# Reordered end of attention, and two experts gathering a third batch of rows on TensorE, in a one-core kernel of expert layer, attention and expert layer

## The chip, the core and the metric

One core of one Trainium2 chip runs the whole program. The metric is the device time of one execution in microseconds, the median of several runs. TensorE is written PE, VectorE DVE, ScalarE ACT, GpSimd POOL and SyncE SP, and the DMA queues that SP and POOL feed are theirs.

## The reference

Four sequences of 512 tokens of 128 numbers go through three residual blocks. `layernorm` is over the last axis.

```
x = x + 0.5 * ffn(layernorm(x))      # 8 experts, each token goes to its best one
x = x + attn(layernorm(x))           # 16 heads of 64, causal, tanh on q, k, v and on the output
x = x + 0.5 * ffn(layernorm(x))      # the same experts and weights again

ffn(t):                              # 2048 tokens, capacity 320 tokens an expert
    probs = softmax(t @ gate_w.T);  e = argmax(probs)
    rank  = how many earlier tokens chose e;  kept if rank < 320
    h = relu(t @ w1[e] + b1[e]);  y = h @ w2[e] + b2[e]
    return probs[e] * y if kept else 0
attn(t):
    q, k, v = tanh(t @ Wq + bq), tanh(t @ Wk + bk), tanh(t @ Wv + bv)
    p = softmax(causal(q @ k.T / 8));  return tanh((p @ v) @ Wo + bo)
```

## The kernel before, in words

There are 16 tiles of 128 tokens (`NT`), four to a batch (`GT`), so `NG` is 4 batches, one for each sequence. The program is written out in full for each engine, instruction after instruction, and engines meet only through the semaphores in `S`; nothing reorders what is written, so an engine that waits holds all that stands behind it.

**Routing.** For each batch DVE takes the largest logit (`choose`), PE counts tokens before each one (`rank_batch`), DVE adds these counts (`take_ranks`) and works out a slot number (`place`, into `idx`, and with `near=True` into `spot` as well). POOL then scatters the rows of `X` to their slots in a table in HBM, `disp`, with four indirect DMAs a batch (`batch_dispatch`; `dispatch_tile` does one tile). SP loads an expert's rows from it (`load_tokens`): 256 rows into `XE[e]`, the other 64 of two experts into `XR[e // 2]` with two DMAs.

**Experts.** `experts(phase)` stands on PE, ACT, DVE, POOL and SP. For an expert `e`, PE turns the normalised rows (`tokens`), DVE copies them to SBUF as `xeT`, PE multiplies by `W1` (`hidden`, four products of 320 columns), ACT applies relu, PE multiplies by `W2` (`outputs`, four more), ACT adds the bias, PE turns the result back (`turn_back`), DVE scales it and adds the row (`Y`), and POOL scatters the rows to the output. Experts 0 and 1 do not wait for the table: PE multiplies normalised tokens (split in a high part `NH` and a low part `NL`, both 16-bit) by matrices of ones and zeros, `HOT[e]`, that DVE writes from `spot` (`hot`); this is `gather`. In phase 0 it covers all four batches. In phase 1 (the last block) it covers only the last batch; the rows of the first three are loaded from the table (`normalise_part` on DVE, five transposes on PE, three copies on ACT in `keep_part`) and are added by DVE when it copies the gathered columns to `xeT` (`gathered`).

**Attention.** A batch has 8 pairs of heads, 32 pairs in all, numbered 0 to 31. On PE, `step` of pair i projects it (`kq`, `v`), scores pair i - 1, mixes pair i - 2 (`context`, once for each head, 30 products) and turns pair i - 3 (`context_t`). ACT takes exponentials (`exps`), DVE makes the 16-bit high part of them (`p_high`), DVE and POOL the low part (`p_low`), and DVE divides the mixed heads by their sums (`normalise`). All `context` results go to one PSUM bank, `cx`, so `context` waits until `normalise` of the head before is done. After 8 pairs, `project_out` multiplies by `Wo` (eight products, one for each pair), ACT takes the tanh, `turn_out` turns it, and DVE adds it to `X` (`add_out`). Then the batch is normalised (`batch_stats`, POOL's `inv_std`, `norm_batch`), turned and routed for the last block. The routing of batches 0 to 2 lies inside the attention of a later batch; that of batch 3 (`NG - 1`) and the scatter of batch 2 stand at the end. `keep_busy` issues products whose result nobody reads.

SP's queue stands in this order at that end: it waits until the scatters of three batches have landed, loads `XE[0]`, `XR[0]` and `XE[1]`, stores batch 3 of `X`, and waits for all sixteen scatters before it loads the rest.

## Time and profile before

| what | us |
|---|---|
| median of three runs | 463.94 |
| the three runs | 464.33, 463.94, 460.05 |
| the profiled execution | 467.87 |
| its span, first to last instruction | 466.1 |
| PE busy in the span | 401.8 (86%) |
| DVE busy in the span | 315.9 (68%) |

Span and rows below are of the profiled execution alone. It is 3.93 us longer than the median of the runs, and 1.77 us of it lies outside the span. Times in rows are microseconds from the start of the span. Up to about 96 us the kernel is in the first expert block, up to about 400 in attention, and after that in the last expert block.

### The profile page before, as it was taken

The page shows a single profiled execution, that of the slowest core. Times are in us where ns is not written, and L with a number is a line of the kernel's source. Part 1 is how long each engine was busy: PE and PEld are TensorE (multiplying, and loading weights), DVE is VectorE, ACT ScalarE, POOL GpSimd, SP SyncE. Part 2 cuts the span into 40 slices and gives each one's busy share as a digit, 9 for nine tenths or more (in the row PEclk, how much of TensorE's full clock was granted, in tenths as well). Part 3 has the DMA queues.
Part 4 walks back from the last instruction along what each step waited for, and adds up shares of the span by engine and source line. Part 5 has one row for each costly group of instructions (what it writes and reads, how often), then busy time and mean ns, then how long its engine had stood idle before and what let it go on. Part 6 is the DMA issues. An engine that isn't in the chain of part 4 may idle for free.

```text
span 466.1 us, 11355 instructions
## 1 busy us (share of the span) xinstructions
PE 401.8 (86%) x4614; PEld 301.9 (65%) x4614; DVE 315.9 (68%) x833; ACT 248.1 (53%) x369; POOL 206.7 (44%) x175
## 2 busy tenths in 40 slices
PE   1689899239899999999999999999999987788992
PEld 0556577115678888587877587877587864345771
DVE  5789655734999776489799379799379793453321
ACT  2111454005787778377778377778377750224541
POOL 6565154702554344154444267443257443030546
PEclk9999999856999999999999999999999998989997
DMA  7912642180000000000000010000010000116531
GB/s 210 367 47 76 176 143 91 35 293 5 1 1 3 1 3 4 0 25 1 3 2 2 7 30 8 9 2 1 7 30 9 9 1 25 52 39 170 158 102 36
DMA packets 25372, 25.46 MB, mean 55 GB/s; under 512 B 2664, under 2 KB 21551, under 8 KB 25048
## 3 DMA queue, kind: packets, MB, share of 16 engines
q1 hardware_dynamic: 21424, 18.33, 13.2%
q0 software_dynamic: 2304, 4.25, 2.8%
q10 hardware_dynamic: 1592, 2.14, 1.3%
q8 instruction: 37, 0.61, 0.5%
q14 instruction: 15, 0.12, 0.1%
HBM read 16.72 MB, written 9.58 MB: 56 GB/s over the span
## 4 chain that ended last, share of the span: by engine, by line
PE 59%; DVE 24%; issue 6%; DMA 4%; POOL 3%; ACT 1%; ACTq 1%; another core or an unknown queue 1%; DVEq 0%; POOLq 0%; SPq 0%
PE sc L795 8%; DVE Pl L1245 6%; PE pj L764 6%; PE sc L663 6%; PE pj L672 6%; DVE Ph L1240 6%; PE tT L844 4%; PE cx L827 4%; PE cx L829 3%; PE pj L774 3%; PE cx L828 3%; PE tT L606 3%; PE pj L795 2%; PE sc L788 1%; POOL out L361 1%
## 5 line engine op out<-in xcount | busy, mean ns | idle before, releaser
L795 PE MATMUL sc<-Tq,Tk 64*128 64x128 f32 (+2 forms) x640 | 78.6, 345 | 0.0
L827 PE MATMUL cx<-Vh,Ph 128*128 128x65 f16 x640 | 65.8, 196 | 10.7 <-DVE cn L1254 6.1
L1240 DVE CAST Ph<-Pf 128x1024 f16<-128x1024 f32 (+1 forms) x48 | 49.7, 1035 | 29.9 <-ACT Pf L551 29.8
L795 PEld LDWEIGHTS sc<-Tq,Tk 64*128 64x128 f32 x640 | 62.3, 187 | 11.6
L827 PEld LDWEIGHTS cx<-Vh,Ph 128*128 128x128 f16 x640 | 58.6, 98 | 16.6 <-DVE cn L1254 7.9
L828 PE MATMUL cx<-Vl,Ph 128*128 128x64 f16 x640 | 65.5, 194 | 0.0
L829 PE MATMUL cx<-Vh,Pl 128*128 128x65 f16 x640 | 65.3, 194 | 0.0
L828 PEld LDWEIGHTS cx<-Vl,Ph 128*128 128x128 f16 x640 | 59.0, 99 | 0.3
L829 PEld LDWEIGHTS cx<-Vh,Pl 128*128 128x128 f16 x640 | 59.1, 98 | 0.0
L462 ACT ACTIVATE hT<-sc,RT 128x320 f32<-128x320 f32 x64 | 33.8, 528 | 34.1 <-PE sc L663 21.7
L382 POOL TENSOR_TENSOR Vl<-Tv,Vh 128x512 f16<-128x512 f32 x16 | 19.2, 1201 | 68.7 <-ACT Vh L543 68.6
L1240 DVE CAST Ph<-Wf 128x1024 f16<-128x1024 f32 (+1 forms) x48 | 42.4, 884 | 5.8 <-ACT Wf L551 5.8
L382 POOL TENSOR_TENSOR Pl<-Wf,Ph 128x1024 f16<-128x1024 f32 x16 | 34.9, 2180 | 19.8 <-DVE Ph L1240 19.8
L382 POOL TENSOR_TENSOR Pl<-Pf,Ph 128x1024 f16<-128x1024 f32 x16 | 34.2, 2138 | 18.2 <-DVE Ph L1240 18.1
L529 ACT ACTIVATE Tk<-pj,RT,am 128x512 f32<-128x512 f32 x32 | 24.9, 777 | 31.9 <-PE pj L764 31.9
L551 ACT ACTIVATE Wf<-sc,pshift 128x1024 f32<-128x1024 f32 x32 | 35.7, 1115 | 10.0 <-PE sc L795 7.3
L663 PE MATMUL sc<-xeT,W 128*128 128x320 f32 x128 | 37.5, 436 | 3.8 <-issue 2.9
L795 PE MATMUL pj<-Tq,Tk 64*128 64x128 f32 x256 | 38.8, 272 | 0.0
L551 ACT ACTIVATE Pf<-sc,pshift 128x1024 f32<-128x1024 f32 x32 | 35.3, 1113 | 6.0 <-PE sc L795 3.8
L382 POOL TENSOR_TENSOR Vl<-Wf,Vh 128x512 f16<-128x512 f32 x16 | 20.3, 1272 | 37.7 <-ACT Vh L543 37.7
L672 PE MATMUL pj<-hT,W 128*128 128x320 f32 x128 | 36.8, 433 | 0.0
L348 POOL DMA_INDIRECT disp<-X,idx x24 | 24.5, 1021 | 27.0 <-DVE idx L1012 14.2
(224 smaller groups left out, 1041.2 us busy)
## 6 DMA issues: line engine op xcount, KB each, us to landing
W<-in_L_ffn_w SPq DMA_DIRECT2D x32, 256.0 KB
disp<-empty SPq DMA_DIRECT2D x2, 1320.0 KB, 7.4
XE<-disp SPq DMA_DIRECT2D x18, 132.0 KB, 2.5
X<-xmid SPq DMA_DIRECT2D x4, 256.0 KB, 4.2
out<-X SPq DMA_DIRECT2D x4, 256.0 KB
XR<-disp SPq DMA_DIRECT2D x18, 33.0 KB, 2.2
X<-in_L_attn_states SPq DMA_DIRECT2D x2, 256.0 KB, 3.3
X<-in_L_attn_states SPq DMA_DIRECT2D x1, 512.0 KB, 5.3
```

The costliest lines, as they stand in the source:

```text
L382: pool.tensor_tensor(dst, src, hi, ALU.subtract).then_inc(done, 1)
L462: act.activation(hT[e % 2][:, ft, :], hbank[ft][:, 0:CAP], ACT.Relu, bias=RT[:, B1_COL + k:B1_COL + k + 1]).then_inc(S["h_ready"], 1)
L551: act.activation(Pf[u][:, :, at], source, ACT.Exp, scale=0.125, bias=pshift[:]).then_inc(S["exp_done"], 1)
L663: mm(hbank[ft][:, 0:CAP], W1[e % 2][:, P * ft:P * ft + P], xeT[e % 2][:], start=True, stop=True).then_inc(S["h_ps"], 1)
L672: last = mm((pj0, pj1)[e % 2][:, 0:CAP], W2[e % 2][:, ft, :], hT[e % 2][:, ft, :], start=ft == 0, stop=ft == FT - 1)
L764: last = mm(ps[:], wpart(w, wl, r), (XL if xl else XH)[:, bass.ds(GN * b, GN)], start=t == 0, stop=t == 2)
L795: m = mm(score_bank(h, c)[:, o + x:o + y], Tk[u][half(h), q:q + P], Tq[u][half(h), q + x:q + y], start=False, stop=last and (c, h) != (2, 0))
L827: mm(cx[:, o:o + HD + 1], Ph[u][:, h, a:a + P], Vh[u][:, kt, h, :], start=kt == 0, stop=False)
L828: mm(cx[:, o:o + HD], Ph[u][:, h, a:a + P], Vl[u][:, kt, h, :], start=False, stop=False)
L829: last = mm(cx[:, o:o + HD + 1], Pl[u][:, h, a:a + P], Vh[u][:, kt, h, :], start=False, stop=kt == qt)
L1240: dve.tensor_copy(Ph[u][:, :, at], Pf[u][:, :, at]).then_inc(S["p_hi"], 1)
L1245: dve.tensor_tensor(Pl[u][:, :, at], Pf[u][:, :, at], Ph[u][:, :, at], ALU.subtract).then_inc(S["p_lo_v"], 1)
```

## The change

1. In the last block experts 0 and 1 now gather batch 2 as well as batch 3 (`gather_group`). Each expert has its own PSUM bank for it (`gbank`: `pj1` and `cx`). The rows of batches 0 and 1, loaded from the table, are multiplied by an identity into the same bank between the two gathers, so that `keep_part`, `part` and the additions of DVE are gone. `normalise_part` stands before the last two `normalise` calls. SP loads these rows once eight tiles (`PART`) are scattered, not twelve.
2. For that, DVE's routing of batch 2 is split (`weigh`, `read_ranks`) and the part that can wait, with `place`, `low_n` and both `hot`, stands behind the last `normalise`, in front of `add_out`. POOL scatters batch 2 behind the `inv_std` of batch 3.
3. At the end of attention PE scores pair 31 before it ranks batch 2, projects four pairs (was six) before `context` of pair 31, and the second head of pair 31 goes to bank `sc[0]`, so that it waits for no `normalise`. `keep_busy(20)` becomes 6.
4. In `experts` PE does both gathers first. In phase 1 it then does `hidden(0)`, `hidden(1)`, `outputs(0)`, `outputs(1)` before `tokens(2)`; in phase 0 a quarter of the second gather stands before `hidden(0)`. In phase 0 DVE's `scale_weights` stands behind the copies of `tokens(2)`.
5. The 64-row loads of two experts (`XR`) are one DMA, not two. `NH`, `NL` and the second `HOT` move to other SBUF tiles (`XH`, `XL`, and a part of `Wf` in phase 1).

```diff
+                    pair = d[e * CAP:(e + 2) * CAP, :].rearrange("(h c) d -> h c d", h=2)
+                    sp.dma_start(XR[e // 2][:], pair[:, MAIN:CAP, :]).then_inc(xr_in[e // 2], 16)
...
-                            sp.wait_ge(S["scattered"], 16 * (2 * NT - GT))
+                            sp.wait_ge(S["scattered"], 16 * (NT + PART))
...
-            batch_dispatch(NG - 2)
             batch_inv_std(NG - 1)
             for e in range(2):
                 pool.wait_ge(xe_in[e], 32)
-            pool.wait_ge(xr_in[0], 64)
+            pool.wait_ge(xr_in[0], 32)
+            batch_dispatch(NG - 2)
             batch_dispatch(NG - 1)
...
+            def gather_group(phase, e, g):
+                since = g - NG + 2
+                done = NG + since + 1 if phase else g + 1
+                pe.wait_ge(S["n_hi"], done)
+                pe.wait_ge(S["n_lo"], done)
+                pe.wait_ge(S["hot_ready"], 2 * NG + 2 * since + e + 1 if phase else NG * e + g + 1)
+                for t in range(GT * g, GT * g + GT):
+                    begin, final = t == (PART if phase else 0), t == NT - 1
+                    mm(gbank[e][:, 0:CAP], NH[:, t, :], HOT[phase][e][:, t, :], start=begin, stop=False)
+                    last = mm(gbank[e][:, 0:CAP], NL[:, t, :], HOT[phase][e][:, t, :], start=False, stop=final)
...
-            step(NG, 0, project=False, route=lambda: rank_batch(NG - 2, cx), cx_read=(S["rank_read"], NS + NG - 1))
             pairs = NPAIR * NG
+            scores(pairs - 1, 1, False)
+            pe.wait_ge(S["ctxn"], 2 * (pairs - 3) + 2)
+            rank_batch(NG - 2, cx)
+            pe.wait_ge(S["rank_read"], NS + NG - 1)
+            context(pairs - 2, 0, 0)
+            context_t(pairs - 3, 1)
+            context(pairs - 2, 0, 1)
             pe.wait_ge(S["tv"], pairs)
-            project_out(NG - 1, pj0, 0, 6)
+            project_out(NG - 1, pj0, 0, 4)
+            context(pairs - 1, 1, 0)
             context_t(pairs - 2, 0)
-            context(pairs - 1, 1, 0)
-            context(pairs - 1, 1, 1)
-            project_out(NG - 1, pj0, 6, 7)
+            context(pairs - 1, 1, 1, sc[0])
+            project_out(NG - 1, pj0, 4, 7)
             context_t(pairs - 1, 1)
             project_out(NG - 1, pj0, 7, 8)
             turn_out(NG - 1)
-            keep_busy(20)
+            for e in range(2):
+                gather_group(1, e, NG - 2)
+            pe.wait_ge(S["part_in"], 1)
+            for e in range(2):
+                rest = slice(REST * e, REST * e + REST)
+                for j in range(2):
+                    mm(gbank[e][:, P * j:P * j + P], XM[e][:, j, :], identf[:], start=False, stop=False)
+                last = mm(gbank[e][:, MAIN:CAP], XMR[rest, :], identf[rest, rest], start=False, stop=False)
+            last.then_inc(S["part_ps"], 1)
+            keep_busy(6, sc[0])
...
-            step(NG, 0, between=lambda: take_ranks(s, NS + NG - 2, GT * (NG - 2), 0, GT, cx))
-            place(s, GT * (NG - 2), 0, GT)
+            step(NG, 0, between=lambda: read_ranks(s, NS + NG - 2, 0, GT, cx))
+            normalise_part()
             normalise(NPAIR * NG - 1, 1, 0)
-            normalise(NPAIR * NG - 1, 1, 1)
+            normalise(NPAIR * NG - 1, 1, 1, sc[0])
+            weigh(s, NS + NG - 2, GT * (NG - 2), 0, GT)
+            place(s, GT * (NG - 2), 0, GT, near=True)
+            low_n(NG, NG - 2)
+            dve.wait_ge(S["spot_ready"], NS + 1)
+            for e in range(2):
+                hot(1, e, NG - 2)
             add_out(NG - 1)
             batch_stats(NG - 1)
             norm_batch(NG, NG - 1)
-            normalise_part()
```

PE at the end of attention, before, from the last product of `context` of pair 30: `L844` is `project_out`, `L606` on `cn` is `context_t`, `L827` the first product of a `context`, `L852` is `turn_out`, `L601` is `keep_busy`. In brackets stands what a row waits for.

```order
L829 MATMUL cx<-Vh,Pl 128x65
L844 MATMUL pj<-CT,Wf 128x512 [waits ct_ready,tv]
L844 MATMUL pj<-CT,Wf 128x512 x5
L606 MATMUL tT<-identf,cn 128x128 [waits ct_ready,ctxn]
L606 MATMUL tT<-identf,cn 128x128 x3
L827 MATMUL cx<-Vh,Ph 128x65 [waits p_lo_v,ctxn,p_lo_p,v_lo]
...
L827 MATMUL cx<-Vh,Ph 128x65 [waits ctxn]
...
L844 MATMUL pj<-CT,Wf 128x512 [waits ct_ready]
L606 MATMUL tT<-identf,cn 128x128 [waits ct_ready,ctxn]
```

The same place after (`L851` is `project_out`, `L834` the first product of a `context`, `L600` on `cn` is `context_t`):

```order
L851 MATMUL pj<-CT,Wf 128x512 [waits ct_ready,tv]
L851 MATMUL pj<-CT,Wf 128x512 x3
L834 MATMUL cx<-Vh,Ph 128x65 [waits p_lo_v,ctxn,p_lo_p,v_lo]
...
L600 MATMUL tT<-identf,cn 128x128 [waits ct_ready,ctxn]
L600 MATMUL tT<-identf,cn 128x128 x3
L834 MATMUL sc<-Vh,Ph 128x65
...
L851 MATMUL pj<-CT,Wf 128x512 [waits ct_ready]
L851 MATMUL pj<-CT,Wf 128x512 x2
L600 MATMUL tT<-identf,cn 128x128 [waits ct_ready,ctxn]
```

Two products of `project_out` moved behind `context`, and the second head's `context` writes `sc` and waits for nothing.

DVE at the same end, before, from the low part of pair 31 (`L1245`) to the sum of batch 3 (`L1278`); `L1012` writes `idx`, `L1254` is the division in `normalise`:

```order
L1245 TENSOR_TENSOR Pl<-Wf,Ph 128x2x256
L1005 TENSOR_REDUCE base<-bases 128x4
...
L1012 TENSOR_TENSOR idx<-sk,tok 128x4
L1250 RECIPROCAL rden<-cx 128x4
L1254 TENSOR_TENSOR cn<-cx,rden 128x4x64
L1250 RECIPROCAL rden<-cx 128x4
L1254 TENSOR_TENSOR cn<-cx,rden 128x4x64
L1278 TENSOR_TENSOR X<-X,tT 128x4x128
```

And after (`L1061`, `L1065` are `normalise_part`, `L1010` begins `weigh`, `L1047` is `low_n`, `L1052` is `hot`, `L1298` the sum):

```order
L1265 TENSOR_TENSOR Pl<-Wf,Ph 128x2x256
L1061 TENSOR_SCALAR XM<-XE 128x128 x4
L1065 TENSOR_SCALAR XMR<-XR 128x128
...
L1274 TENSOR_TENSOR cn<-sc,rden 128x4x64
L1010 TENSOR_TENSOR bases<-ebase,mask 128x32
...
L1038 TENSOR_TENSOR idx<-sk,tok 128x4
L1040 TENSOR_TENSOR spot<-sk,tok 128x4
L1047 TENSOR_TENSOR XL<-XN,XH 128x512
L1052 TENSOR_SCALAR Pf<-order,spot 128x320 x4
L1052 TENSOR_SCALAR Wf<-order,spot 128x320 x4
L1298 TENSOR_TENSOR X<-X,tT 128x4x128
```

The slot numbers of batch 2 moved behind the last division, and the hot tiles of batch 2 now stand between that and the sum.

PE at the start of the last block, before, from the second gather on (`L663` is `hidden`, `L672` is `outputs`, `L651` and `L653` are `tokens`, `L683` is `turn_back`):

```order
L672 MATMUL pj<-hT,W_0 128x320 [waits h_ready,w2_in0]
L672 MATMUL pj<-hT,W_0 128x320 [waits h_ready] x3
L663 MATMUL sc<-xeT,W_1 128x320 [waits h_ready,xe_ready,w1_in1]
L663 MATMUL sc<-xeT,W_1 128x320 [waits h_ready] x3
L651 MATMUL tT<-identf,XM 128x128 [waits xe_ready,xm_ready]
...
L663 MATMUL sc<-xeT,W_0 128x320 [waits h_ready,xe_ready,w1_in0]
...
L651 MATMUL tT<-identf,XM 128x128 [waits xe_ready,xm_ready]
L651 MATMUL tT<-identf,XM 128x128
L672 MATMUL pj<-hT,W_1 128x320 [waits h_ready,w2_in1]
```

And after (`L660` is `hidden`, `L669` is `outputs`, `L648` is `tokens`):

```order
L660 MATMUL sc<-xeT,W_0 128x320 [waits xe_ready,w1_in0]
L660 MATMUL sc<-xeT,W_0 128x320 x3
L660 MATMUL sc<-xeT,W_1 128x320 [waits h_ready,xe_ready,w1_in1]
L660 MATMUL sc<-xeT,W_1 128x320 [waits h_ready] x3
L669 MATMUL pj<-hT,W_0 128x320 [waits h_ready,w2_in0]
L669 MATMUL pj<-hT,W_0 128x320 [waits h_ready] x3
L669 MATMUL pj<-hT,W_1 128x320 [waits h_ready,w2_in1]
L669 MATMUL pj<-hT,W_1 128x320 [waits h_ready] x3
L648 MATMUL tT<-identf,XM 128x128 [waits xe_ready,xm_ready]
```

`outputs(1)` moved from behind `tokens(3)` to before `tokens(2)`.

## Rows read from the trace of the kernel before

**Rows 1.** The profile page: shares of the chain that ended last, by engine.

```profile
PE 59%; DVE 24%; issue 6%; DMA 4%; POOL 3%; ACT 1%; ACTq 1%; another core or an unknown queue 1%; DVEq 0%; POOLq 0%; SPq 0%
```

**Rows 2.** PE in order of time: start, length, line, count, idle before.

```profile
376.51 0.19 PE L621 MATMUL cx<-mask,lower 128*128 128x32 bf16 x1 [0.99 <-DVE cn L1254]
...
380.55 0.20 PE L827 MATMUL cx<-Vh,Ph 128*128 128x65 f16 x1 [0.82 <-DVE carry L999]
...
383.36 5.40 PE L844 MATMUL pj<-CT,Wf 128*128 128x512 f32 x12
...
389.90 0.19 PE L829 MATMUL cx<-Vh,Pl 128*128 128x65 f16 x1
...
392.92 0.23 PE L827 MATMUL cx<-Vh,Ph 128*128 128x65 f16 x1 [2.83 <-DVE cn L1254]
```

**Rows 3.** DVE in order of time, at the end of attention.

```profile
379.50 0.18 DVE L992 TENSOR_TENSOR bases<-ebase,mask 128x32 f32<-128x32 f32 x1
...
380.11 0.18 DVE L998 TENSOR_TENSOR pos<-cx,carry 128x32 f32<-128x32 f32 x1
...
386.52 0.18 DVE L1005 TENSOR_REDUCE base<-bases 128x4 f32<-128x32 f32 x1
...
392.15 0.18 DVE L1250 RECIPROCAL rden<-cx 128x4 f32<-128x4 f32 x1 [4.27 <-remote]
```

**Rows 4.** The chain that ended last, in order of time: start, length, what.

```profile
394.74 1.78 PE pj L844 x2
396.52 0.45 PE tT L606 x4
...
400.24 0.69 DVE X L1278
...
405.48 0.64 PE tT L606 x4
...
416.29 2.70 DMA disp<-X,idx
419.00 4.21 DMA XE<-disp
```

**Rows 5.** Windows: busy time of each engine, then granted clock, DMA share, GB/s.

```profile
393.00:394.00 1.00, 1.00 (x20) 1.00 (x21) 0.00 (x0) 0.00 (x0) 0.46 (x1) 0.50 0.10 16
...
410.00:411.00 1.00, 1.00 (x4) 0.30 (x2) 0.86 (x8) 0.00 (x0) 0.00 (x0) 0.50 0.00 0
```

**Rows 6.** PE and DVE in order of time, from 400 us on.

```profile
400.04 4.48 PE L601 MATMUL cx<-lower,onesb 128*128 128x512 bf16 x20
...
405.25 1.11 DVE L1035 TENSOR_SCALAR XM<-XE 128x128 f32<-128x128 f32 x4
...
411.60 0.94 DVE L1026 TENSOR_SCALAR Pf<-order,spot 128x320 f16<-128x320 f16 x4
...
424.16 0.44 PE L651 MATMUL tT<-identf,XM 128*128 128x128 f32 x2 [1.38 <-DVE XMR L1058]
...
428.77 0.60 DVE L1053 TENSOR_SCALAR XM<-XE 128x128 f32<-128x128 f32 x2 [3.40 <-DMA XE<-disp]
...
430.58 2.39 PE L663 MATMUL sc<-xeT,W 128*128 128x320 f32 x8
```

**Rows 7.** POOL and SP in order of time.

```profile
34.08 1.38 POOL L348 DMA_INDIRECT disp<-X,idx  x1 [0.30 <-issue]
...
402.55 1.04 POOL L342 TENSOR_TENSOR r<-ve,mhalf 128x4 f32<-128x4 f32 x1 [9.09 <-DVE ve L953]
412.41 1.04 POOL L348 DMA_INDIRECT disp<-X,idx  x1 [8.82 <-DVE idx L1012]
...
425.99 1.09 SPq L254 DMA_DIRECT2D XR<-disp  x2
```

**Rows 8.** PE, then DVE in order of time, in the first block.

```profile
39.12 2.39 PE L663 MATMUL sc<-xeT,W 128*128 128x320 f32 x8 [0.74 <-DVE xeT L1071]
...
53.89 0.60 DVE L1053 TENSOR_SCALAR XM<-XE 128x128 f32<-128x128 f32 x2 [2.51 <-DMA XE<-disp]
```

More of the change, by code:

```diff
@@ L589, in _ @@
             exp_logits(NS - 1 + NG, 0, GT)
-            keep_part()
             experts(1)
@@ L684, in turn_back @@
                     last.then_inc(S["back_ps"], 1)
-                gather(0)
-                hidden(0)
-                gather(1)
-                outputs(0)
-                hidden(1)
+                if phase:
+                    gather(0, (NG - 1,))
+                    gather(1, (NG - 1,))
+                    hidden(0)
+                    hidden(1)
+                    outputs(0)
+                    outputs(1)
+                else:
+                    gather(0, range(NG))
+                    gather(1, (0,))
+                    hidden(0)
+                    gather(1, range(1, NG))
+                    outputs(0)
+                    hidden(1)
                 tokens(2)
@@ L695, in experts @@
                     tokens(e + 2)
-                    outputs(e)
+                    if e > 1 or not phase:
+                        outputs(e)
                 outputs(E - 2)
```

119 lines of the change are left out of this document (50 added, 69 removed).

## The prediction, made before the changed kernel ran

> **What bounds the kernel now.** I read the chain that ended last first. It is mostly PE and DVE, with DMA, waits of an unknown source and POOL as small parts [rows 1]. The change leaves the bulk of attention alone, so three places count, and for each I followed PE, DVE, POOL and SP in order of time.
>
> The end of attention is a chain that alternates between PE and DVE. PE waits 0.99 for DVE's division before it ranks batch 2, then 0.82 before `context` of pair 30, for `carry`, which DVE writes behind four instructions of weights [rows 2, 3]. `context` of pair 31, first head, ends at 390.09 (389.90 + 0.19), and DVE begins to divide it only at 392.15, with a wait whose source the profile calls remote. So PE starts the second head at 392.92 after 2.83 idle [rows 2, 3]. [...] The sum of batch 3 comes at 400.24, its turned rows at 405.48 [rows 4].
>
> From there the chain is routing, POOL's four scatters, 2.70 to land, and 4.21 until `XE[2]` is loaded [rows 4]. PE is idle 1.38 before `tokens(2)` [rows 6]. Next the load of `XE[4]` ends a DVE wait at 428.77, and `hidden(3)` begins at 430.58 [rows 6]. From there to the last experts PE hardly stops.
>
> In the first block PE waits 0.74 before `hidden(0)`, and later `XE[4]` ends a DVE wait at 53.89 [rows 8].
>
> **Part A, the first block.** Eight of the 32 products of the second gather move before `hidden(0)`. In phase 1 one expert's gather issues every 0.136 (an estimate from starts 0.13 to 0.14 apart), so eight are 1.1. They cover the wait of 0.74 and end 0.15 to 0.2 later than `hidden(0)` could have begun. What follows on PE comes 0.9 earlier: 1.1 less 0.2. `hidden(1)` sends SP to the next loads, so `XE[4]` also comes 0.9 earlier, and the DVE wait of [rows 8] moves with it. The later `scale_weights` and the single `XR` DMA lie beside other work there. I take -0.9. Bounds: 0, if DVE's maxima of the weights, which stand before the copy of the second gather, end too late, and -1.3, if `XE[4]` gains from SP too.
>
> **Part B, the end of attention.** Times are those of the trace before. The scores of pair 31 fill the wait of 0.99 and cost nothing. The four DVE instructions of `weigh` (379.50 to 380.11, 0.6 [rows 3]) leave the path of `carry`, so `context` of pair 30 starts at 380.0, not 380.55, and DVE ends the low part of pair 31 0.55 earlier, at 386.05. PE is free at 383.36 - 0.5 = 382.85. Eight passes of `project_out` at 5.40 / 12 = 0.45 [rows 2] last until 386.45. Then `context` (30 products at 0.03, with its end 1.0), `context_t` 0.45 [rows 4], the second head without a wait 1.0, and six passes 2.7: 391.6. From the start of the last `context_t` to the sum it takes 400.24 - 396.52 = 3.7 [rows 4]: 395.3. The sum comes 5.0 earlier.
>
> These 5.0 have two parts. If DVE had answered at 390.1, the end of the products, and the clock had stayed at full, the profiled execution would have saved 2.0 of the wait, 0.9 in 30 products and 0.9 in the two passes (1.78 against 2 x 0.45), 3.8 in all. The other 1.2 is what the order saves in any execution. The new order needs no answer between the heads, so it takes both.
>
> The cover is thin in two places. DVE from 386.05: `normalise_part` 1.4 (1.11 [rows 6] and one tile of 0.3), the divisions, the second ending at 389.7 (0.8 after the products end at 388.9), then `weigh` 0.6, `place` 387.88 - 386.52 = 1.4 [rows 3], `low_n` 0.7, two `hot` 1.9 (twice 0.94 [rows 6]): 394.3. That is 1.0 before the sum could start; any more on DVE is paid in full. PE after `turn_out`, 395.7: 16 products 2.2, the identity products 1.1 (ten passes at most 0.11 each, from 0.44 for two turned tiles of two, ends overlapping [rows 6]), six filler products at 4.48 / 20 = 0.22 [rows 6], 1.35: 400.3. The turned rows are due at 405.48 - 5.0 = 400.5. The five transposes of `XM` that go, and the copies of ACT, lay beside DVE's choice and give nothing. `normalise_part` lay beside PE's turning and gives nothing either.
>
> POOL: `inv_std` runs 5.0 earlier, 397.55 to 398.6 [rows 7]. Behind it stand the four scatters of batch 2, 1.29 apart ((416.29 - 412.41) / 3 [rows 4, 7]), until 403.7. Behind them wait those of batch 3, due at 412.41 - 5.0 = 407.4. So 3.7 are free, and they cost nothing.
>
> Part B is -5.0. Bounds: -1.2 where the execution had no such wait, and -5.3.
>
> **Part C, the last block.** In the wait for the table PE now does both gathers and two experts in full. Counted on the old times: gathers until 415.2, then four times 2.15 (2.39 with the end [rows 6]) until 423.9. `tokens(2)` stood at 424.16 [rows 6], so `outputs(1)` fits with 0.2 to spare. It used to lie behind `tokens(3)`, where PE waited for DVE, and so for `XE[4]`, anyway. It gives nothing by itself: `hidden(3)` starts 1.8 after `XE[4]` lands, whatever PE does. What moves `XE[4]` is SP: two pairs of `XR` loads stand before it, 1.09 a pair [rows 7], and each becomes one load, so it is issued 1.1 earlier. The weights before it share its DMA engines, so I take half, -0.6. Bounds 0 and -1.1. After it the chain is PE's and carries the gain to the end.
>
> **The sum.** -0.9 - 5.0 - 0.6 = -6.5. Against the profiled execution, 467.87, that is 461.4. It stands 3.93 above the median. Either profiling adds this in any execution, the wait at 390 included in both, and then the forecast is 463.94 - 6.5 = 457.4. Or the median has no such wait, and then it is 463.94 - 0.9 - 1.2 - 0.6 = 461.2. For the first speaks that the runs are themselves 3.9 apart (464.33 and 463.94 against 460.05), close to 3.8: two with the wait and one without. For the second speaks that 467.87 - 463.94 is close to 3.8 as well. I hold the first as likelier, since it also explains the lowest run. The forecast is 457.4.
>
> **Rivals.** *The wait was an accident of the profiled execution*: 461.2, within 1%. The trace shows no second one like it in some 400 handovers, which speaks for it.
>
> *PE's clock falls early.* PE will be idle for about 0.9 and 1.1 around the last pair (an estimate, from the 3.7 less its own work of 1.8), and it was granted 0.50 after idle times of 2.83 and again at 410 [rows 2, 5]. At half speed the gather, identity and filler products take 9.3, not 4.65, and end at 405.0, 4.5 after the rows are due: 457.4 + 4.5 = 461.9. Against: the same idle times stood there before, with the clock at full.
>
> *POOL is late with eight scatters* (the slower case). A scatter beside DVE's hot tiles took 1.38 [rows 7], not 0.96. Four such last 1.7 longer, less than the 3.7 free. If instead DVE holds POOL off altogether, the scatters of batch 2 start only when the last hot tile is written, about 413.5 - 5.0 = 408.5, and the last of eight is issued at 408.5 + 7 x 1.29 = 417.5 against 416.29 - 5.0 = 411.3. That is +6.2 on the chain: 463.6, or 461.2 + 6.2 = 467.4 where the wait was an accident, slower than before. It decides from the point where the four scatters of batch 2 take over 8.8 us (398.6 to 407.4) instead of 5.2.
>
> [...]
>
> *The order doesn't shorten the end*, because DVE's hot tiles come late: if the 4.6 us of DVE work after the division grow by 2, the sum starts 1.0 later, 458.4. This lies in the range.
>
> **How the numbers follow.** Forecast case 0.50; the accident 0.32; early clock loss 0.09; POOL late 0.09. The low end takes the outer bounds, 463.94 - 1.3 - 5.3 - 1.1 = 456.2, and 0.7 for a further wait of this kind gone: 455.5. The high end holds the accident with A at a third of its size and C at nothing, 463.94 - 0.3 - 1.2 = 462.4, the clock case, and 0.3 for thin cover: 462.7. Outside lie the POOL case and a few per cent on either side. About 1%, 4.6 us, is what a measurement of this kernel tells from no change. Faster by more than that is below 459.3: the forecast case and a little of the others, 0.52. Slower by more is above 468.6: the upper part of the POOL case and the unforeseen, 0.06. Within 1%: 0.42.
>
> **What would show it.** In the profile after: no DVE wait between the two heads of pair 31, and the second head's products straight behind `context_t`; full clock until past 400; the sum of batch 3 near 394.4 (395.3 less the 0.9 of part A), with DVE done with the hot tiles shortly before; POOL's eight scatters with a gap between the fourth and the fifth; PE nearly without idle time before `tokens(2)`; `XE[4]` landing about 9.1 after the scatters have, where it was 9.8. A DVE wait of the remote kind at another place, the gather at half clock, or hot tiles later than yT would make the prediction wrong.

## The result, and the profile after

The changed kernel took 467.1 us (median of 20 runs), the kernel before 463.72 beside it. The ratio is 1.0079, with a 95% interval of 1.0055 to 1.0102: 0.8% slower, within the 1% that the prediction called no change, but above its whole range of 455.5 to 462.7.

The profiled execution after has a span of 465.3 and took 467.4. Lines of its page, in order of the page: the packets of SP's queue, the chain that ended last by engine, and the loads from the table with KB each and the median us to landing (the page gives none for the merged `XR`).

```profile
q1 hardware_dynamic: 21154, 18.33, 13.1%
...
PE 60%; DVE 22%; issue 7%; POOL 5%; DMA 4%; ACT 1%; ACTq 1%; SPq 0%; DVEq 0%; POOLq 0%
...
XE<-disp SPq DMA_DIRECT2D x18, 132.0 KB, 4.2
...
XR<-disp SPq DMA_DIRECT2D x9, 66.0 KB
```

The same lines of the kernel before (its chain is in [rows 1]):

```profile
q1 hardware_dynamic: 21424, 18.33, 13.2%
...
XE<-disp SPq DMA_DIRECT2D x18, 132.0 KB, 2.5
...
XR<-disp SPq DMA_DIRECT2D x18, 33.0 KB, 2.2
```

The nine `XR` loads replace eighteen, as they should. But the loads of `XE`, which the change doesn't touch, now take 4.2 to land and not 2.5. And the queue has 270 packets fewer, 30 for each merged load. The chain shows where this matters in the first block (start, length, what):

```profile
45.22 4.31 DMA XR<-disp
...
56.26 2.40 issue
58.65 3.80 PE sc L660 x7
```

DVE in order of time, the same place. They answer to the DVE row of [rows 8].

```profile
49.56 0.35 DVE L1084 TENSOR_SCALAR XMR<-XR 128x128 f32<-128x128 f32 x1 [2.10 <-DMA XR<-disp]
...
54.35 0.60 DVE L1079 TENSOR_SCALAR XM<-XE 128x128 f32<-128x128 f32 x2 [2.35 <-DMA XE<-disp]
56.17 0.35 DVE L1084 TENSOR_SCALAR XMR<-XR 128x128 f32<-128x128 f32 x1 [1.22 <-DMA XR<-disp]
```

Before, DVE waited 2.51 for `XE[4]` and then nothing for `XR[2]`. Now it waits 2.35 for `XE[4]` and 1.22 more for `XR[2]`, and earlier 2.10 for `XR[1]`. PE's `hidden(3)` before and after, and windows around the second (each line has the stretch, its length, the busy time of PE, PEld, DVE, ACT and POOL, the granted clock, the DMA share and GB/s):

```profile
56.88 2.39 PE L663 MATMUL sc<-xeT,W 128*128 128x320 f32 x8 [0.42 <-issue]
```

```profile
58.65 4.08 PE L660 MATMUL sc<-xeT,W 128*128 128x320 f32 x8 [2.40 <-issue]
```

```profile
58.00:59.00 1.00, 0.35 (x1) 0.30 (x2) 1.00 (x5) 0.00 (x0) 0.00 (x0) 0.97 0.56 173
59.00:60.00 1.00, 1.00 (x3) 0.68 (x2) 0.96 (x3) 0.18 (x1) 0.90 (x1) 0.50 0.10 31
393.00:394.00 1.00, 1.00 (x4) 0.44 (x3) 0.90 (x7) 0.00 (x0) 0.00 (x0) 1.00 0.00 0
```

`hidden(3)` starts 1.77 later than in [rows 8]'s execution, after 2.40 idle instead of 0.42, and runs 4.08 instead of 2.39, with PE granted 0.50 just behind that idle time (0.97 from 58 to 59, 0.50 from 59 to 62, 0.82 from 62 to 63). The last of the windows shown belongs to the end of attention: it answers to the 0.50 of [rows 5], and the clock there is now at full. DVE at that end, against [rows 3, 4]:

```profile
390.75 0.18 DVE L1270 RECIPROCAL rden<-cx 128x4 f32<-128x4 f32 x1
...
392.13 0.18 DVE L1270 RECIPROCAL rden<-sc 128x4 f32<-128x4 f32 x1 [0.67 <-PE sc L836]
...
395.23 0.93 DVE L1052 TENSOR_SCALAR Pf<-order,spot 128x320 f16<-128x320 f16 x4
396.09 0.93 DVE L1052 TENSOR_SCALAR Wf<-order,spot 128x320 f16<-128x320 f16 x4
398.47 0.69 DVE L1298 TENSOR_TENSOR X<-X,tT 128x512 f32<-128x512 f32 x1 [1.45 <-PE tT L859]
```

The second division waits 0.67, on PE, and the hot tiles are done 1.45 before the sum of batch 3 can start. POOL against [rows 7]:

```profile
402.01 1.03 POOL L349 DMA_INDIRECT disp<-X,idx  x1 [0.20 <-issue]
...
406.07 0.96 POOL L349 DMA_INDIRECT disp<-X,idx  x1 [0.30 <-issue]
410.51 0.96 POOL L349 DMA_INDIRECT disp<-X,idx  x1 [3.48 <-DVE idx L1038]
```

The eight scatters stand as foreseen, 1.33 to 1.38 apart for batch 2, with 3.48 free before those of batch 3. In the last block DVE waits for `XR[1]`, later gets `XE[4]`, and then waits for `XR[2]`; against [rows 6]:

```profile
421.33 0.35 DVE L1084 TENSOR_SCALAR XMR<-XR 128x128 f32<-128x128 f32 x1 [1.58 <-DMA XR<-disp]
...
426.27 0.60 DVE L1079 TENSOR_SCALAR XM<-XE 128x128 f32<-128x128 f32 x2 [3.33 <-DMA XE<-disp]
428.09 0.34 DVE L1084 TENSOR_SCALAR XMR<-XR 128x128 f32<-128x128 f32 x1 [1.22 <-DMA XR<-disp]
```

```profile
429.39 2.39 PE L660 MATMUL sc<-xeT,W 128*128 128x320 f32 x8 [3.52 <-issue]
```

### The profile page after: what moved, and what is told of

Its sections match the earlier page's. It is cut to its first block, busy times and chain, and to the rows that moved or that the text cites. A ratio compares the mean times of both kernels' runs of the same rounds, so it can differ in the third digit from the quotient of the medians.

```text
span 465.3 us, 11366 instructions
## 1 busy us (share of the span) xinstructions
PE 402.4 (86%) x4623; PEld 303.7 (65%) x4623; DVE 318.5 (68%) x841; ACT 247.8 (53%) x367; POOL 206.9 (44%) x175
## 4 chain that ended last, share of the span: by engine, by line
PE 60%; DVE 22%; issue 7%; POOL 5%; DMA 4%; ACT 1%; ACTq 1%; SPq 0%; DVEq 0%; POOLq 0%
PE sc L802 8%; PE sc L660 7%; PE pj L771 6%; PE pj L669 6%; DVE Pl L1265 6%; DVE Ph L1260 6%; PE tT L851 4%; PE cx L834 4%; PE cx L836 3%; PE cx L835 3%; PE pj L781 3%; PE tT L600 3%; POOL disp L349 2%; PE pj L802 2%; PE pj L851 2%
## 5 line engine op out<-in xcount | busy, mean ns | idle before, releaser
L834 PE MATMUL cx<-Vh,Ph 128*128 128x65 f16 x630 | 64.1, 195 | 8.0 <-DVE cn L1274 2.9
L834 PEld LDWEIGHTS cx<-Vh,Ph 128*128 128x128 f16 x630 | 57.3, 97 | 14.4 <-DVE cn L1274 4.8
L835 PE MATMUL cx<-Vl,Ph 128*128 128x64 f16 x630 | 63.8, 193 | 0.0
L836 PE MATMUL cx<-Vh,Pl 128*128 128x65 f16 x630 | 63.6, 193 | 0.0
L835 PEld LDWEIGHTS cx<-Vl,Ph 128*128 128x128 f16 x630 | 57.7, 98 | 0.3
L836 PEld LDWEIGHTS cx<-Vh,Pl 128*128 128x128 f16 x630 | 57.8, 97 | 0.0
L660 PE MATMUL sc<-xeT,W 128*128 128x320 f32 x128 | 38.9, 450 | 7.4 <-issue 7.4
L669 PE MATMUL pj<-hT,W 128*128 128x320 f32 x128 | 36.6, 433 | 0.0
L660 PEld LDWEIGHTS sc<-xeT,W 128*128 128x128 f32 x128 | 24.6, 197 | 18.2 <-issue 9.7
```

The lines of the kernel that those rows point to most:

```text
L660: mm(hbank[ft][:, 0:CAP], W1[e % 2][:, P * ft:P * ft + P], xeT[e % 2][:], start=True, stop=True).then_inc(S["h_ps"], 1)
L669: last = mm((pj0, pj1)[e % 2][:, 0:CAP], W2[e % 2][:, ft, :], hT[e % 2][:, ft, :], start=ft == 0, stop=ft == FT - 1)
L834: mm(bank[:, o:o + HD + 1], Ph[u][:, h, a:a + P], Vh[u][:, kt, h, :], start=kt == 0, stop=False)
L835: mm(bank[:, o:o + HD], Ph[u][:, h, a:a + P], Vl[u][:, kt, h, :], start=False, stop=False)
L836: last = mm(bank[:, o:o + HD + 1], Pl[u][:, h, a:a + P], Vh[u][:, kt, h, :], start=False, stop=kt == qt)
```

## The experiments

Twelve runs were made, in three groups, each beside the kernel before on the same chip. Ratios are against that; each is worked out from all executions and is not the quotient of two medians (run 1's 461.26 stands beside a median of 463.79, which would be 0.9945). Microseconds of gain or loss are worked out from the ratios. XR stands for the load of the 64 rows of two experts.

**Milestones.** Read from the timelines of PE and DVE of each profiled execution. Logits are PE's products for the routing of batch 2, sum is DVE's sum of batch 3 (`X<-X,tT`), `XE[4]` the start of its normalising on DVE (`XM`). The third column is a time from the start of the span, the four behind it are differences of two starts.

| kernel | ratio | hidden(4), first block | logits to sum | sum to hidden(0) | sum to XE[4] | sum to hidden(3) |
|---|---|---|---|---|---|---|
| before, first profile | 1 | 61.92 | 31.79 | 14.75 | 28.53 | 30.34 |
| before, again | 1 | 61.98 | 28.21 | 14.79 | 28.40 | 30.21 |
| changed | 1.0079 | 65.38 | 26.65 | 14.63 | 27.80 | 30.92 |
| changed, XR in two | 0.9965 | 61.37 | 26.65 | 15.90 | 27.56 | 30.85 |
| before, XR in one | 1.0084 | 63.00 | 28.21 | 15.32 | 28.26 | 31.44 |
| before, XR wide | 0.9993 | 61.87 | 28.21 | 15.31 | 27.51 | 29.64 |
| changed, XR wide | 0.9921 | 61.05 | 26.64 | 15.83 | 27.07 | 29.50 |

**1. The changed kernel with XR as two DMAs.**

```diff
-                    pair = d[e * CAP:(e + 2) * CAP, :].rearrange("(h c) d -> h c d", h=2)
-                    sp.dma_start(XR[e // 2][:], pair[:, MAIN:CAP, :]).then_inc(xr_in[e // 2], 16)
+                    for h in range(2):
+                        sp.dma_start(XR[e // 2][REST * h:REST * h + REST, :],
+                                     d[(e + h) * CAP + MAIN:(e + h + 1) * CAP, :]).then_inc(xr_in[e // 2], 16)
...
```

> The changed kernel with the 64-row loads of two experts as two DMAs again, all else as changed. Theory: the single load has an access pattern whose outermost dimension is 2, goes to two of the 16 DMA engines and lands about 4 us after issue instead of 2.1, so experts 2 and 4 of both expert blocks wait for it. Then this kernel gives back 4.3 us in the first block (3.4 by which attention starts late, and the 0.9 of part A that was forecast) and 0.6 in the last: 467.1 - 4.9 = 462.2 us, 461 to 463.5, and the wait of 2.40 before hidden(3) in the first block is about 0.5. Rival: the new order of the gathers and of scale_weights costs the time; then it stays at 466 to 468.

Measured: 461.26 us, ratio 0.9965, interval 0.9944 to 0.9987. One line of the change cost 1.14%, 5.3 us, and without it the change is a gain of 1.6. DVE in the first block, in order of time:

```profile
47.53 0.34 DVE L1085 TENSOR_SCALAR XMR<-XR 128x128 f32<-128x128 f32 x1 [0.48 <-DMA XR<-disp]
...
53.34 0.60 DVE L1080 TENSOR_SCALAR XM<-XE 128x128 f32<-128x128 f32 x2 [2.81 <-DMA XE<-disp]
53.86 0.34 DVE L1085 TENSOR_SCALAR XMR<-XR 128x128 f32<-128x128 f32 x1
```

The wait for `XR[1]` is 0.48 and not 2.10, and that for `XR[2]` is gone, so `hidden(4)` comes 4.0 earlier than in the profile of the changed kernel. The idle time before `hidden(3)` is 1.55, though, not the 0.5 I had expected. And in the last block DVE waits for `XR[2]` with two loads as well:

```profile
421.82 0.35 DVE L1085 TENSOR_SCALAR XMR<-XR 128x128 f32<-128x128 f32 x1 [1.39 <-DMA XR<-disp]
```

Run 6 has such a wait of 1.41, the other profiles with two loads have none there. So in the last block the wait for `XR[2]` alone doesn't tell the two forms apart. The time from issue does: DVE starts on `XR[2]` 5.6 and 6.2 after SP began to issue it in the two blocks of the changed kernel, and 3.6 and 5.0 in this run.

**2. The kernel before with XR as one DMA**, and nothing else of the change.

```diff
-                    for h in range(2):
-                        sp.dma_start(XR[e // 2][REST * h:REST * h + REST, :],
-                                     d[(e + h) * CAP + MAIN:(e + h + 1) * CAP, :]).then_inc(xr_in[e // 2], 16)
+                    pair = d[e * CAP:(e + 2) * CAP, :].rearrange("(h c) d -> h c d", h=2)
+                    sp.dma_start(XR[e // 2][:], pair[:, MAIN:CAP, :]).then_inc(xr_in[e // 2], 16)
...
```

> The kernel before, with the 64-row loads of two experts as one DMA, nothing else. Theory (two engines): the second such load lands about 1.8 us after XE[4] in each block, so hidden(3) starts 1.3 to 1.8 us later in both, and where PE's clock then falls some more: 466.5 to 469 us, against 463.7. Rival (the order costs the time): 463 to 464.

Measured: 466.98 us, ratio 1.0084, interval 1.0053 to 1.0115. That is a price of 3.9 us without the rest of the change; given the interval (2.5 to 5.3) it can't be told from the 5.3 of run 1. DVE in the last block:

```profile
418.76 0.35 DVE L1057 TENSOR_SCALAR XMR<-XR 128x128 f32<-128x128 f32 x1 [1.26 <-DMA XR<-disp]
...
423.55 0.60 DVE L1052 TENSOR_SCALAR XM<-XE 128x128 f32<-128x128 f32 x2 [3.18 <-DMA XE<-disp]
425.43 0.35 DVE L1057 TENSOR_SCALAR XMR<-XR 128x128 f32<-128x128 f32 x1 [1.28 <-DMA XR<-disp]
```

Both `XR` waits are there, 1.26 and 1.28, and `hidden(3)` starts 1.1 to 1.2 later after the sum than in the two profiles of the kernel before. In the first block it starts 1.0 to 1.1 later in the span. I had expected 1.3 to 1.8 in each.

**3. The kernel before, once more.**

> The kernel before, unchanged, for a second profile. If the DVE wait of 4.27 us between the two heads of pair 31 is how this kernel runs, it stands in this profile too, with half clock after it. If it was an accident of the first profiled execution, DVE answers at once and the span is 3.5 to 4 us shorter.

Measured: 462.52 us in its one run, span 460.7, which is 5.4 shorter, more than the 3.5 to 4 expected. DVE at the end of attention:

```profile
388.41 0.18 DVE L1250 RECIPROCAL rden<-cx 128x4 f32<-128x4 f32 x1 [2.26 <-PE cx L829]
...
390.31 0.18 DVE L1250 RECIPROCAL rden<-cx 128x4 f32<-128x4 f32 x1 [1.18 <-PE cx L829]
...
394.94 0.69 DVE L1278 TENSOR_TENSOR X<-X,tT 128x512 f32<-128x512 f32 x1 [4.00 <-PE tT L852]
```

Both divisions wait on PE, 2.26 and 1.18, where [rows 3] has one wait of 4.27 called remote. The sum comes 28.21 after the logits, not 31.79. The profiles of runs 2 and 9, which keep the old order, give 28.21 as well: one of the four profiles with the old order has the wait.

**4. The changed kernel with one XR load in another form ("wide").** Rows of the two experts alternate, so that the outermost dimension is 64, not 2. ACT then adds the bias in two instructions an expert, and PE's turning reads in a strided order.

```diff
-                    pair = d[e * CAP:(e + 2) * CAP, :].rearrange("(h c) d -> h c d", h=2)
-                    sp.dma_start(XR[e // 2][:], pair[:, MAIN:CAP, :]).then_inc(xr_in[e // 2], 16)
+                    pair = d[e * CAP:(e + 2) * CAP, :].rearrange("(h c) d -> c h d", h=2)
+                    sp.dma_start(XR[e // 2][:], pair[MAIN:CAP, :, :]).then_inc(xr_in[e // 2], 16)
...
```

> The changed kernel with a single load of the 64-row parts whose outermost dimension is 64: the rows of the two experts come interleaved, PE writes them back in order when it turns them, and ACT writes its last 64 columns interleaved, in two instructions in place of one. Theory (number of engines): the load lands in 2 to 2.5 us as the two did, SP saves 1.1 us before XE[4], and the time is that of the two-load kernel less 0 to 1: 461 to 462.5. Rival (any one DMA of 128 such rows is slow): 466 to 468.

Measured: 459.93 us, ratio 0.9921, interval 0.9892 to 0.9951. Its page:

```profile
q1 hardware_dynamic: 21280, 18.33, 13.3%
...
XE<-disp SPq DMA_DIRECT2D x18, 132.0 KB, 2.8
...
XR<-disp SPq DMA_DIRECT2D x9, 66.0 KB, 2.9
```

One load of the same 66 KB now lands in 2.9 (median) where the first one in the chain above took 4.31, and the `XE` loads are back at 2.8. The landing is slower than the 2 to 2.5 expected, the time better than the 461 to 462.5. The packets fit: two DMAs a pair became one, and 16 packets fewer a pair are left, 144 in all. The form with outermost 2 left out 30, as if each load ended with 2 packets and not 16 (my estimate from the 270 and 144 that are fewer on nine loads).

The DMA share tells the two forms apart as well. In the changed kernel it is 0.15, with 40 and 37 GB/s, from 54.00 to 54.50 and from 54.50 to 55.00, while `XR[2]`, issued at 50.56, is on its way. In this run it is 0.67, with 175 GB/s, from 48.50 to 48.75, while `XR[0]`, issued at 46.86, is. Of 16 DMA engines that is 2.4 and 10.7, an estimate from these shares: near the two engines of the expectation of run 1 for the first form, and more for the wide one. The packets and the landing times agree. How the form decides on the number, no run shows, nor how much each DMA engine carried.

**5. The changed kernel with XR in two, and `outputs(1)` back behind `tokens(3)`.**

```diff
                     outputs(0)
-                    outputs(1)
...
-                    if e > 1 or not phase:
-                        outputs(e)
+                    outputs(e)
```

> The changed kernel with XR as two DMAs again (461.3 us as such), and outputs(1) back at its old place behind tokens(3) in the last block. My theory: moving it gives nothing by itself, so 461.3 within the measurement; hidden(2) about 2.2 earlier than there, hidden(3) at the same time, since XE[4] sets it. Rival: the move saves its 2.2 us of PE work, and undoing it costs them: about 463.5. Second rival: the work put back fills the idle time before hidden(3) and keeps the clock at full there, so that hidden(3) takes 2.39 and not 3.33: about 460.4.

Measured: 461.13 us, ratio 0.9966, interval 0.9937 to 0.9995, against 0.9965 without it. `hidden(2)` starts 23.85 after the sum and not 25.77, `hidden(3)` 30.39 and not 30.85. Moving `outputs(1)` gives nothing that the time can tell. The second rival looks to the idle time and the clock. In run 1, with `outputs(1)` ahead, PE is idle before `hidden(3)` and the clock falls while it runs (1.00 from 423 to 424, then 0.72, then 0.50):

```profile
423.12 3.33 PE L661 MATMUL sc<-xeT,W 128*128 128x320 f32 x8 [2.25 <-issue]
```

It is 3.33 long, against 2.39 with the work behind. But the other profiles with `outputs(1)` ahead ran it in 2.39 too (after 3.52 idle in the changed kernel, 2.97 in run 6, 0.97 in runs 4 and 7), so the half clock is that execution's and not shown to come from the order. `hidden(3)` stands 29.51 to 30.85 after the sum in runs 1, 6 and 7, and the 30.39 of this run lies within that.

**6. The changed kernel with XR in two, and the second gather of the first block whole behind `hidden(0)`.**

```diff
-                    gather(1, (0,))
                     hidden(0)
-                    gather(1, range(1, NG))
+                    gather(1, range(NG))
```

> The changed kernel with XR as two DMAs again (0.9965 of the kernel before, 461.3 us), and the second gather of the first block whole behind hidden(0), as before. Theory, part A as I predicted it: the eight products ahead of hidden(0) cover a wait of 0.74, so without them hidden(0) comes 0.2 earlier and outputs(0) 0.9 later: ratio 0.998, 462.2 us. Rival: XE[4] sets hidden(3) of the first block, whatever stands before, so the move gives nothing: 461.3, ratio 0.9965.

Measured: 461.26 us, ratio 0.9964, interval 0.9938 to 0.9991. The rival holds. `hidden(2)` does start 1.0 later after `hidden(0)` (12.14 against 11.10), but `hidden(4)` stands at 61.49, against 61.37 in run 1.

**7. The changed kernel with XR in two, and the second head of pair 31 back in `cx`.**

```diff
-            context(pairs - 1, 1, 1, sc[0])
+            context(pairs - 1, 1, 1)
...
-            normalise(NPAIR * NG - 1, 1, 1, sc[0])
+            normalise(NPAIR * NG - 1, 1, 1)
```

> The changed kernel with XR as two DMAs again (0.9965 of the kernel before, 461.3 us), and the second head of the last pair back in the bank cx, so that its context waits for DVE's division of the first head. Theory, part B as I predicted it: between the heads four products for context_t stand already, so the wait is the division less these, about 0.3: 461.6, ratio 0.997. The sum of batch 3 then comes 26.8 after the logits of batch 2 (26.5 without). Rival: the bank is what made the end of attention 1.7 shorter in the profiles: sum 28.2 after these logits and 463.0, ratio 1.000.

Measured: 462.23 us, ratio 0.9977, interval 0.9945 to 1.0008. The sum comes 27.16 after the logits, between the 26.65 of the new order and the 28.21 of the old: the bank is 0.5 of the 1.56, the rest of the order 1.05. I had expected 26.8, the rival 28.2. The time can't tell this: the interval takes in run 1's ratio.

**8. The changed kernel with the wide load, and DVE normalises expert e+4 behind `tokens(e+3)`.**

```diff
-                for e in range(E):
-                    if e + 2 < E:
-                        tokens(e + 2)
-                    if e == 0 and between:
-                        between()
-                    if e + 4 < E:
-                        normalise_rows(e + 4)
-                    if phase == 0:
-                        split_weights(e)
-                    outputs(e)
+                tokens(2)
+                if between:
+                    between()
+                for e in range(E):
+                    outputs(e)
+                    if e + 3 < E:
+                        tokens(e + 3)
+                    if e + 4 < E:
+                        normalise_rows(e + 4)
+                    if phase == 0:
+                        split_weights(e)
```

> The changed kernel with one interleaved XR load (459.9 us as such), and one edit more: DVE normalises the loaded rows of expert e+4 behind tokens(e+3), not before it, so that the copy of the columns for hidden(3) no longer waits for XE[4], in both expert blocks. Theory: the load of XE[4] ends the wait before hidden(3) in both blocks. PE is idle 0.77 and 0.97 there, with the clock at full in the profile, so up to 1.7 go, and as XE[4] must then only be ready for hidden(4) they stay gone: 458.2 to 458.9. Rival: hidden(4) now waits for the same load, one expert later, and nothing is gained: 459.9. Slower case: the normalising now lies on the way of the copies of the next expert, 0.6 each, and costs: 460.5.

Measured: 456.67 us, ratio 0.9892, interval 0.9852 to 0.9932. The first block shows it. `hidden(3)` with the wide load alone, then with this edit:

```profile
56.01 2.39 PE L664 MATMUL sc<-xeT,W 128*128 128x320 f32 x8 [0.77 <-issue]
```

```profile
54.63 2.32 PE L664 MATMUL sc<-xeT,W 128*128 128x320 f32 x8
```

`hidden(4)` stands at 59.60, not 61.05. The ratios are 1.3 us apart, within the 1.0 to 1.7 expected, but their intervals overlap, so the time alone doesn't show the gain. In the last block the idle time before `hidden(3)` stays 0.97: there DVE's scaling and the copy are what is late (run 12).

**9. The kernel before with the wide load**, edit as in run 4.

> [...] Theory: the single load costs only through its spread over two DMA engines; spread over all, it frees 0.5 of SP for each pair: 0.6 to 1.2 faster than the kernel before, so 462.6 to 463.2 against 463.8. Rival: a single load is no gain in any form, since XE[4] lands when the engines are free: 463.8. Slower case: rows of 512 bytes in a stride order are slow, or ACT's bias in two instructions costs: 465 or more.

Measured: 462.53 us, ratio 0.9993, interval 0.9964 to 1.0023. In time the wide load gives the kernel before nothing that can be told (0.6 to 1.2 us were expected, and the interval allows them), but the price of run 2 is gone: the two intervals don't touch. DVE in the last block:

```profile
414.99 0.35 DVE L1061 TENSOR_SCALAR XMR<-XR 128x128 f32<-128x128 f32 x1
...
420.10 0.60 DVE L1056 TENSOR_SCALAR XM<-XE 128x128 f32<-128x128 f32 x2 [3.42 <-DMA XE<-disp]
420.93 0.35 DVE L1061 TENSOR_SCALAR XMR<-XR 128x128 f32<-128x128 f32 x1 [0.23 <-DMA XR<-disp]
```

`XR[2]` is waited for 0.23, not 1.28, and `XE[4]` comes 27.51 after the sum, 0.9 sooner than in run 3. No run shows the load spread over all engines, as the theory has it: the 0.67 of run 4 is an estimated 10.7 of 16.

**10. The changed kernel with the wide load, and nine products nobody reads** in PE's gaps while batch 3 is routed.

```diff
             turn_batch(NG - 1)
+            keep_busy(3, sc[0])
             route_logits(NG - 1, sc[1])
+            keep_busy(6, sc[0])
             rank_batch(NG - 1, sc[3])
```

> The changed kernel with one interleaved XR load (459.9 us as such), and nine products whose result nobody reads: three behind the turning of batch 3 and six behind its logits, where PE is idle 0.69 and 1.40. Theory: these gaps, with those before, make the clock fall at about 400.5, and the gather of batch 3 runs at half clock until 407.1; with PE busy there the clock stays at full and hidden(0) of the last block comes 2.9 earlier (14.6 to 14.8 after the sum of batch 3, where it was 17.7): 457.0 us. Rival: the clock falls all the same, for work done before, as it fell in the kernel before with its twenty such products: 459.9. Second rival: the clock is kept there and lost later, in the next wait before tokens(3): 458.5.

Measured: 459.73 us, ratio 0.9923, interval 0.9889 to 0.9957, against 0.9921 without. Windows of run 4's kernel, then of this one; the granted clock is the third number from the end:

```profile
401.00:402.00 1.00, 0.93 (x10) 0.49 (x11) 0.86 (x8) 0.00 (x0) 0.00 (x0) 0.50 0.20 68
405.00:406.00 1.00, 1.00 (x5) 0.60 (x4) 0.30 (x2) 0.00 (x0) 0.69 (x2) 0.50 0.21 72
```

```profile
401.00:402.00 1.00, 1.00 (x7) 0.54 (x7) 0.56 (x3) 0.21 (x1) 0.70 (x1) 1.00 0.20 68
405.00:406.00 1.00, 0.00 (x0) 0.00 (x0) 0.96 (x6) 0.00 (x0) 0.27 (x1) 1.00 0.00 0
```

The clock is kept, and `hidden(0)` comes 14.62 after the sum, not 15.83. (I had put this at 2.9 earlier; the trace had 1.2 to give.) It gains nothing, since `XE[4]` comes 27.06 after the sum, as before (27.07), and `hidden(3)` stands behind it:

```profile
420.76 0.60 DVE L1085 TENSOR_SCALAR XM<-XE 128x128 f32<-128x128 f32 x2 [2.67 <-DMA XE<-disp]
```

**11. Runs 8 and 10 together.**

> One interleaved XR load, DVE's normalising of expert e+4 behind tokens(e+3) (both together 0.9892 of the kernel before), and the nine products in PE's gaps while the last batch is routed. These alone kept the clock at full in the profile (hidden(0) 14.6 after the sum, where it was 15.8 with the clock lost), but gained nothing in the time, since XE[4] came 27.07 after the sum in both and hidden(3) waited for it. Theory: with hidden(3) free of XE[4] the 1.2 stay gained wherever the clock used to fall: 0.2 to 1.2 us faster than without the products, ratio 0.987 to 0.989. Rival: the clock was at full for the gather without them in that profile, so they give nothing: 0.9892. Slower case: hidden(2) and hidden(3) now wait longer for XE[2], which the scatters set: 0.9892 as well, with a longer idle time before hidden(2).

Measured: 456.7 us, ratio 0.9875, interval 0.9833 to 0.9917. The interval takes in 0.9892. The sum to `hidden(3)` is 28.28, as in run 8 (28.29), in whose profile the clock was back at full when the gather began (granted 0.50 from 401 to 403, 0.52 to 404 and 1.00 after, the gather at 404.43). So the fillers stay unproven, though the ratio lies in the 0.987 to 0.989 expected.

**12. Run 11, and `tokens(e+2)` before `turn_back(e-1)`** on PE, with DVE's copy before its scaling.

```diff
-                    turn_back(e - 1)
                     tokens(e + 2)
+                    turn_back(e - 1)
...
-                    outputs(e)
                     if e + 3 < E:
                         tokens(e + 3)
+                    outputs(e)
```

> As the run with both edits and the nine products, and besides tokens(e+2) stands before turn_back(e-1) on PE, and DVE copies these columns before it scales the rows of the expert turned back. Theory: PE is idle 0.97 before hidden(3) of the last block, 0.53 of it DVE's scaling and 0.22 the turning, which leave the path: 0.5 to 0.75 us faster, ratio 0.001 to 0.0016 lower. Elsewhere outputs(e) covers that handover, so nothing changes. Rival: the turned results come later to DVE and POOL, and the last rows are scattered later: 0.3 slower.

Measured: 455.39 us, ratio 0.9843, interval 0.9797 to 0.9889. PE's `hidden(3)` of the last block in run 11, then in this one:

```profile
418.82 2.39 PE L664 MATMUL sc<-xeT,W 128*128 128x320 f32 x8 [0.97 <-issue]
```

```profile
417.26 2.39 PE L664 MATMUL sc<-xeT,W 128*128 128x320 f32 x8 [0.34 <-issue]
```

The idle time fell by 0.63, as expected, and `hidden(3)` comes 0.62 sooner after the sum. The intervals of runs 11 and 12 overlap, so this step is seen in the trace and not in the time. The whole version is 1.6% faster than the kernel before.

## Why the prediction was wrong

**The step that failed** is the one on the loads: in part A "the single `XR` DMA lie[s] beside other work there", and in part C "each becomes one load, so it is issued 1.1 earlier", worth -0.6. I took for granted that a DMA of twice the rows takes no longer than its halves, and looked at it only through SP's time. In this form it costs about 5.3 us. It lands late, and holds DVE up by 1.22 behind `XE[4]` in both blocks, and by 2.10 and 1.58 before it.

In the first block `hidden(3)` starts 2.3 later than in run 1, of which 0.6 is how much later `hidden(0)` of this execution began. The idle time of 2.40 is followed by half clock (0.50 from 59 to 62), 1.7 more. In the last block `hidden(3)` stands 0.07 to 1.41 later after the sum than in the four profiles with two loads (runs 1, 5, 6, 7: 30.85, 30.39, 30.31, 29.51). Together that is 3.5 to 4.8. Up to 0.6 more may belong to the load, since run 5's `hidden(0)` began 0.44 later than run 1's and its `hidden(3)` only 0.17. The ratios of the changed kernel and run 1 give 5.3.

Runs 1, 2, 4 and 9 show the cause from four sides: the load in that form costs 5.3 us in the changed kernel and 3.9 in the one before, and in the wide form nothing in either (0.9921 against 0.9965, and 0.9993).

The -0.6 itself looks as if it had come true, and that is luck: `XE[4]` came 0.6 to 0.7 sooner after the sum (27.80 against 28.40 and 28.53), but in run 1, without the merged load, it came sooner still (27.56), and in run 2, with nothing but the merged load, only 0.1 to 0.3 sooner (28.26). The merged load brings `XE[4]` forward by 0.5 to 0.9 only in the wide form (27.07 against 27.56, 27.51 against 28.40).

**The base was the wrong one of two.** The forecast of 457.4 held that the median contained the wait at 390, because the runs are 3.9 apart. Three of four profiles with the old order (runs 2, 3 and 9) don't have it, so it isn't how the kernel usually runs. The rival *the wait was an accident* gave 461.2, and without the load the kernel took 461.26. That this is so close is partly luck: 461.2 held 0.9 of part A and 0.6 of part C, which gave nothing, and the gain by the ratio is 1.6, not 2.7. The *POOL is late* rival named 467.4, near the 467.1 measured, and that is luck altogether, since no scatter was late. What spreads the runs is seen elsewhere. Windows from 100 to 150 us, of the kernel before (first profile), the changed one, and run 9's:

```profile
100.00:150.00 50.00, 43.73 (x553) 32.38 (x551) 39.24 (x101) 32.02 (x44) 20.16 (x14) 0.87 0.11 41
```

```profile
100.00:150.00 50.00, 42.17 (x485) 29.73 (x487) 37.62 (x106) 28.99 (x40) 18.14 (x12) 0.83 0.18 60
```

```profile
100.00:150.00 50.00, 43.96 (x604) 33.32 (x604) 42.87 (x106) 34.77 (x48) 20.61 (x14) 0.98 0.11 42
```

From `hidden(4)` to the sum of batch 0, at 205.53, 209.22 and 201.81 in these three, it is 143.6, 143.8 and 139.9 us, with a mean clock of 0.87, 0.83 and 0.98. The other eleven profiles give 140.9 to 144.1, nearly in the order of their clock (0.96 to 0.87), whatever the kernel. The next two batches are steady: sum 0 to sum 2 takes 140.4 to 140.8 in these three. The executions without a profile agree: each has a mean clock over its span on record, and in the 19 of the kernel before beside runs 1 to 4 the fastest, 459.70, has 0.973 and the slowest, 464.87, has 0.958. So a low run like the 460.05 needs no wait at 390 to explain it. The clock of that one run is not on record, and that the clock sets the time, and not both something else, is argued.

**Part A**, -0.9: nothing. The products ahead of `hidden(0)` did bring `hidden(2)` forward, by 0.8 in the span (49.80 in run 1, 50.59 in run 6), but `hidden(3)` hangs on `XE[4]` and its rows, which hardly moved. The step "`hidden(1)` sends SP to the next loads, so `XE[4]` also comes 0.9 earlier" is wrong in its end: SP issued these loads 0.6 earlier in run 1, but DVE took `XE[4]` at 53.34 there and at 53.45 in run 6.

**Part B**, -5.0 against the profiled execution, of it 1.2 in any: right. From the logits to the sum 31.79 became 26.65, -5.1; against run 3 it is -1.6, 0.4 more than I had. The second head's own bank is a third of it (run 7). The half clock that Part B counts on is seen in [rows 4, 5]: the two products of `project_out` take 1.78 at a granted 0.50, and in run 3 the same two take 0.94 at 1.00. The clock at full until past 400, the hot tiles ready before the sum and the free time of POOL are all in the profile. Neither *the clock falls early* nor *POOL is late* came true in the changed kernel: its clock fell only after 407, was 0.50 from 408 to 410, 0.75 in the next microsecond and at full from 411, and the gather of batch 3 began at 410.93. In variants (runs 1, 4, 5 and 7) it fell some 8 to 9 us after the sum and stayed down for 6 to 7 us (in run 1, with the sum at 392.27, it was 0.77 from 400 to 401, 0.50 from 401 to 407 and 0.82 from 407 to 408): `hidden(0)` came 15.8 to 15.9 after the sum and not 14.63, so it cost 1.2, not 4.5. The clock came back in the middle of the gather, which ran from 404.72 to 408.17 in run 1. That DVE can hold POOL off altogether, as one case of the *POOL is late* rival has it, no run shows. For batch 2 no row here bears on it, since the hot tiles ended at 397.02 and the first scatter began at 402.01. But DVE writes batch 3's hot tiles from 409.82 to 411.71:

```profile
409.82 0.96 DVE L1052 TENSOR_SCALAR Pf<-order,spot 128x320 f16<-128x320 f16 x4
```

The scatter at 410.51, beside them, took 0.96, no longer than the three after it. So this DVE work held no scatter off.

**Part C.** `outputs(1)` by itself gives nothing: right (run 5). The -0.6 on `XE[4]` matched by luck, and the load that was to give it is what cost the time, as above. The weights before `XE[4]` and the loads themselves do fill the DMA engines together: in the kernel before, the DMA share is 1.03, 1.06 and 0.99 in the half microseconds from 426.0 to 427.5, with weights issued at 423.86 and 424.49 and two `XE` loads from 425.04 on. That this halves the gain of an earlier issue was my guess, and no run shows it.

With the runs' values the sum is A 0, B -1.6, the load +5.3: 463.7 + 3.7 = 467.4, against 467.1 measured. This is no test of the 5.3, which is itself the difference of the changed kernel and run 1. What it tests is B: 1.6 by the sums in the traces, and 1.6 by the ratio of run 1, whose interval allows 0.6 to 2.6.

## What to carry to other kernels

Count a DMA by how long it takes to land as well as by what it moves: two loads that become one save SP's time, 1.09 to 0.50 here, but the form with outermost size 2 took 4.31 to land and the one with 64 took 2.9 (median), and the `XE` loads beside them 4.2 and 2.8. So look at the landing times in a profile, those of the loads behind it too. A wait in one profile that the profile can't name should be looked for in a second profile of the same kernel before a forecast leans on it. And when a stage waits for a chain of loads, bringing PE's work forward gains nothing until what waits for the last load is itself moved back (run 8, then 12).
